# Selective scan's fourth silu of a block, from behind the gathered experts' gelu to in front of it in ScalarE's order

## What is computed

```python
# selective scan
xs, gate = jnp.split(h @ W_in, 2, axis=-1)
xs = silu(causal_conv(xs) + conv_b)                 # 512 channels, kernel 4
delta = mean(softplus(xs @ Wd + bd), axis=-1)
dA = exp(delta * A);  Bx = (xs @ B_mat.T) * delta
hs = scan(h = dA * h + Bx)
y = (hs @ C_mat.T + D_vec * xs) * silu(gate)
out_1 = x + y @ W_out
# experts: 8 heads, one of 4096 experts each
indices, scores = product_key_top1(x @ Wq.T, keys)
gate = relu(scores)
lin = (x . in_a[indices]) * gate
hidden = gelu(x @ W_in.T + sum_h lin * in_b[indices])
lout = (hidden . out_a[indices]) * gate
out_2 = hidden @ W_out.T + sum_h lout * out_b[indices]
```

## Time and profile before

| | |
|---|---|
| median of 3 runs | 4099.81 us (4099.64 to 4100.76) |
| the profiled execution's own time | 4113.66 us |
| its span, first to last instruction | 4111.9 us |
| TensorE busy, and its mean granted clock | 3689.5 us (90%), 0.943 of full speed |
| VectorE busy | 2578.5 us (63%) |
| ScalarE busy | 1742.1 us (42%) |
| GpSimd busy | 1087.5 us (26%) |
| the woven part of layer 1 in the span | about 1017 to 2110 us |

### The profile page before, as it was taken

The page is one execution under the profiler, slowest core; times in us unless marked ns, Lnnn a source line. Parts: engine busy times, 40 slices in busy tenths (PEclk is TensorE's granted clock), DMA queues, the critical chain, the costliest instruction groups (busy, mean ns, idle before and its releaser), DMA issues.

```text
span 4111.9 us, 47352 instructions
## 1 busy us (share of the span) xinstructions
PE 3689.5 (90%) x16820; PEld 2091.3 (51%) x16820; DVE 2578.5 (63%) x6523; ACT 1742.1 (42%) x3213; POOL 1087.5 (26%) x1140
## 2 busy tenths in 40 slices
PE   8899999787999898898859999999899999999997
PEld 7477777445544444454435555565543443444332
DVE  3534343646888977787754344442587888778881
ACT  2344333232343334333423333332226766666767
POOL 0611111602555545454512222222111010011001
PEclk7999999888999999899979999999899999999999
DMA  4356554204555646555510000000000000000000
GB/s 153 136 173 207 202 203 159 78 29 138 185 186 188 209 155 185 183 188 181 185 69 3 0 0 1 1 0 0 21 1 1 1 1 1 16 6 1 1 1 21
DMA packets 96157, 356.61 MB, mean 87 GB/s; under 512 B 15440, under 2 KB 42720, under 8 KB 85936
## 3 DMA queue, kind: packets, MB, share of 16 engines
q0 software_dynamic: 57328, 301.90, 22.6%
q1 hardware_dynamic: 37504, 49.58, 3.6%
q10 hardware_dynamic: 1088, 2.10, 0.1%
HBM read 322.32 MB, written 31.20 MB: 86 GB/s over the span
## 4 chain that ended last, share of the span: by engine, by line
PE 62%; DVE 24%; ACT 7%; issue 3%; POOL 3%; DMA 1%; POOLq 0%; SPq 0%; ACTq 0%; DVEq 0%
PE ps L171 48%; PE ps L2414 5%; DVE pm L2592 4%; PE ps L1947 2%; DVE gathB L1606 2%; PE ps L1429 2%; DVE hacc L1590 2%; ACT P L2743 2%; DVE mi L1548 2%; DVE ps L2595 1%; POOL xs_sorted L1147 1%; DVE tm L1506 1%; DVE fa L1856 1%; PE ps L2000 1%; DVE mx L1544 1%
## 5 line engine op out<-in xcount | busy, mean ns | idle before, releaser
L2743 ACT ACTIVATE P<-ps 128x512 f32<-128x512 f32 (+3 forms) x1280 | 589.2, 548 | 202.2 <-PE ps L171 199.5
L2592 DVE TENSOR_REDUCE pm<-ps 128x1 f32<-128x512 f32 x768 | 484.1, 685 | 82.1 <-PE ps L171 78.8
L1745 POOL DMA_INDIRECT gathB<-in_tab,idx x256 | 280.9, 1097 | 455.7 <-PE ps L1429 386.5
L2791 POOL TENSOR_SCALAR_AFFINE_SELECT P<-P 128x256 f32<-128x256 f32 x256 | 103.3, 407 | 911.0 <-ACT P L2743 907.1
L1745 POOL DMA_INDIRECT gathA<-in_tab,idx x256 | 272.8, 1066 | 226.9 <-DVE gte L1562 149.3
L171 PE MATMUL ps<-KS,QS 64*128 64x512 f32 (+3 forms) x1280 | 304.2, 424 | 21.4 <-DVE QS L2575 4.9
L2414 PE MATMUL ps<-P,Va 128*32 128x512 f32 (+3 forms) x2560 | 300.0, 541 | 11.3 <-POOL P L2791 6.3
L171 PE MATMUL ps<-QS,KS 64*128 64x512 f32 (+3 forms) x1280 | 283.4, 412 | 10.2 <-DVE xT L2543 4.6
L171 PEld LDWEIGHTS ps<-KS,QS 64*128 64x128 f32 x1280 | 139.7, 184 | 252.7 <-DVE pm L2592 69.5
L171 PE MATMUL ps<-f,K 128*128 128x512 f32 x1024 | 253.4, 399 | 13.9 <-POOL f L2205 11.3
L2595 DVE CUSTOM_DVE_ANT_0 ps<-ps,past 128x128 f32<-128x128 f32 (+3 forms) x512 | 240.7, 514 | 38.7 <-PE ps L171 37.6
(11 more groups left out here) (366 smaller groups left out, 7172.5 us busy)
## 6 DMA issues: line engine op xcount, KB each, us to landing
xs_sorted<-zero SPq DMA_DIRECT2D x1, 9088.0 KB, 33.0
xs<-xs_sorted SPq DMA_DIRECT2D x71, 128.0 KB, 2.2
ys_sorted<-ys SPq DMA_DIRECT2D x71, 128.0 KB, 1.7
gathA<-in_tab,idx POOLq DMA_INDIRECT x256, 5.5
gathB<-in_tab,idx POOLq DMA_INDIRECT x256, 5.1
out<-xT SPq DMA_DIRECT2D x8, 512.0 KB, 3.1
xT<-in_x SPq DMA_DIRECT2D x4, 512.0 KB, 9.6
xT<-in_x ACTq DMA_DIRECT2D x4, 512.0 KB, 8.6
```

The lines of the kernel that those rows point to most:

```text
L1745: pool.indirect_dma_start(out=(GA, GB)[half][:, h, :], out_offset=None, in_=d[f"tab{half}"], in_offset=bass.IndirectOffsetOnAxis(ap=idx[t ...
L2592: v = dve.tensor_reduce(m, p, AX.X, ALU.max)
L2743: act.activation(P_[:, hh, off:BW], psx.tile("s2", j, n, kt, pr, hh)[:, off:BW], ACT.Exp).then_inc(*psx.emptied(MN.act, "s2", j, n, kt, pr ...
L2791: pool.affine_select(out=P_, in_=P_, compare_op=ALU.is_ge, fill=0.0, base=0, pattern=[[0, 2], [1, 128]], channel_multiplier=-1).then_inc(* ...
```

## The change

In `act_mamba` the silu of round 6 (the fourth chunk) is emitted in slot 13, right behind the third chunk's, and no longer in slot 14. Slots 8 to 13 are as before, and so is the number of slots of a block. No instruction, wait or buffer is added or taken out in the program's text; table loads are placed by the compiler from the order.

```diff
@@ -1636,7 +1636,7 @@
                         yield from at.to((2, 3)[slot])
                     for i in range(7):
-                        yield from at.to(8 + i)
+                        yield from at.to(8 + min(i, 5))
                         if i < 4:
                             act.wait_ge(*MA.dve.has("halo", n))
                             act.wait_ge(*MA.pe.has("xs", n, i))
```

## The result

| | before | after |
|---|---|---|
| median of the runs that the prediction was set against | 4100.28 us (4099.64 to 4101.49, 4 runs) | 4072.39 us (4064.61 to 4075.00, 4 runs) |
| ratio, 95% interval | | 0.9928 [0.9911, 0.9946] |
| the profiled execution's own time, and its span | 4113.66, 4111.9 us | 4070.20, 4068.5 us |
| granted TensorE clock, mean | 0.943 | 0.949 |

The kernel is 27.9 us faster (22 to 36 by the interval); 33.9 us and 4065.9 us were forecast.

The account below looks back on a forecast made before the run. The fourth silu, queued behind the gelu's wait on ScalarE, was taken to stall TensorE, then VectorE. Gains of 9.7 + 9.4 + 8.4 + 6.4 = 33.9 us in blocks 3 to 6 gave 4065.9 us, range 4057 to 4075.

Parts of the forecast that it names:

- Where the order changes: Slot counts put the fourth silu ahead of the gelu in blocks 3 to 6 only; silu table loads 13 to 9.
- The silu's own cost: On ScalarE, cost 0, hidden in idle time; gelu not delayed, tightest in block 6 with 2.5 us to spare.
- Block 3, 9.7 us: TensorE's B starts 7.89 us earlier and, at full clock, takes 3.61 instead of 5.46, another 1.85 us.
- Block 4, 9.4 us: B follows routing groups 0 and 1, starting 7.45 us earlier, plus 1.99 us of clock.
- Block 5, 8.4 us: B starts at 1717.8 instead of 1724.17, 6.4 us earlier, plus 1.95 us of clock.
- Block 6, 6.4 us: B starts 6.4 us earlier; 4.4 us of idle time stay, and B is left at 4.91 us.
- What is late next: VectorE still waits about 1.2 us for block 3's group 2; transposes and gathers have slack, so the shift is kept.
- The check by the windows: Blocks 3 to 5 falling to block 2's length, plus block 6: 43.7 us, 4056.1, the gain's far end.
- Clock kept low: Rival: B stays slow after the shorter gaps, so 5.8 us of clock fall out: 4071.7 us; chance 0.08.
- Something else early: Rival: a gather or ScalarE's softplus is late next and takes a third: 22.6 us gained, 4077.2; chance 0.07.
- Loads only: Rival: only 5.1 us of table loads come off, 4094.7 us; chance 0.06 together with no order change.
- Slower: Rival: the silu's wait for the fourth convolution holds up the gelu, 31.6 us lost, 4131.4 us; chance 0.03.

Follow-up runs that it names:

- e3: Fourth silu moved in block 3 alone, blocks 4 to 7 as in the kernel before: 4102.30 us, ratio 0.9981 to the kernel before.
- e4: Fourth silu moved in block 6 alone, against the kernel before: 4104.37 us, ratio 0.9987.
- e5: Kernel before, old order, with a silu replacing the gelu of tiles 13, 17, 21 and 25, so without those table loads: ratio 0.9973 to the kernel before.
- e9: The changed kernel a third time, on another chip: 4147.07 us, ratio 0.9925 to the kernel before.
- e7: The changed kernel with block 7's third and fourth silu also in slot 12, in front of the gelu: ratio 0.9894 to the kernel before.
- e2: The kernel before, unchanged, run again against itself for a second trace: ratio 0.9997.
- e6: The changed kernel with another table loaded ahead of the fourth silu's wait in blocks 3 to 6: 4144.18 us, ratio 0.9901 to the kernel before.

## Why the prediction was right

**What bounds the kernel now: right.** The chain convolution, gelu's wait, silu, B, routing group 2 was the one that set the time. e3 and e4 show it block by block, e5 that it was the wait and not the loads.

**Where the order changes: right.** Blocks 3 to 6 and no other, 9 loads left, as the counts had it.

**The silu's own cost: right.** The gelu's load still starts 0.08 us after the last `hacc` ends (1420.06 + 4.68 = 1424.74, 1424.82). Block 6 was called the tightest, and there too the gelu was not held up: ScalarE still waits 2.44 us for its input after the silu.

**Block 3, 9.7 us: 9.8.** 7.89 us of start (16.77 ahead at B less 8.88 in block 2) and the slow B turned fast, 5.46 to 3.61.

**Block 4, 9.4 us: 12.0.** The term was too small, and its premise failed. B did not follow the routing groups without a wait (0.81 us idle), but TensorE reached them earlier: the products with `dg` before them had come after 2.75 us of idle time and run slowly, and now come after 1.25. Before, then after:

```profile
1563.33 1.63 PE L1429 MATMUL ps<-dg,gathB 128*128 128x128 f32 x8 [2.75 <-ACT dg L1708]
1564.76 1.92 PE L1429 MATMUL ps<-hg,gathB 128*128 128x128 f32 x8
```

```profile
1542.64 1.37 PE L1429 MATMUL ps<-dg,gathB 128*128 128x128 f32 x8 [1.25 <-ACT dg L1708]
1543.85 1.33 PE L1429 MATMUL ps<-hg,gathB 128*128 128x128 f32 x8
```

**Block 5, 8.4 us: 8.9.** The wait is 2.27 us where the prediction had 1.1, for the same reason (the products with `dg` ahead of it came after 2.82 us of idle time before, 1.25 now), and B is fast all the same.

**Block 6, 6.4 us: 5.1.** The start moved as said (4.29 us idle, 4.4 forecast), but B became slower than before, 6.35 against 4.91, with the clock at 0.50 in its first part; the prediction had left it as it was and named a slower B only as its worst case, at 0.69 us; it was 1.44. This term was too large.

```profile
1815.00:1820.00 5.00, 4.01 (x5) 0.73 (x6) 4.86 (x14) 2.24 (x3) 3.79 (x4) 0.50 0.85 275
```

**What is late next: right in its order.** The waits for group 2 are 1.20, 1.21 and 2.77 us in blocks 3 to 5, and 5.52 in block 6, where about 4 was said: the slower B is in it. TensorE's wait for `u` in the four blocks is 7.95 us, where "under 7" was said. The last gather of block 3 is issued at 1436.93, which is the trace's lead of 8.9 us and no more, and the `lin` products at 1445.21 start on ScalarE's `xt_`, as before; no gather became the bound.

**From the blocks to the median.** The sum for the four blocks, 33.9, stands against 35.7 in the first pair of traces and 33.2 between the mean woven parts (two traces of before, three of after 1086.5: 32.6). The three measured differences are 27.9, 36.3 and, for e9, 34.0 between medians. Why the first is smaller is not shown; its four runs span 10 us, and stages that the change doesn't touch vary by several us from run to run. The step that took the profile's sum over to the median one to one was right on average (the three have a mean of 32.7) and is good to about 6 us for one comparison. Part of the agreement is luck: blocks 4 and 6 missed in opposite directions, by 2.6 and 1.3 us in the first pair and by 1.3 and 2.1 in the second, so the sum is closer than its terms. The check by the windows, 43.7 us, was too large: block 5 kept a wait and B in block 6 became slower.

**The rivals.** Clock kept low: not in blocks 3 to 5; in block 6, where the sum had left B slow, it was slower still. Something else early: not seen. Loads only: refuted by e5. Slower: its condition never came near; in e7, where the fourth convolution of block 7 ends late, the gelu still waited 0.86 us for its own input.

## What to carry to other kernels

When two streams are woven into one in-order queue, look for a cheap instruction whose input is ready while the one ahead of it waits, and whose output an engine with more to do is idle for; its price is that engine's wait, not the instruction's or its table load's. Check a static weave over its whole length: two periods of 68 and 68.48 steps drift, so the same code is in one order in blocks 0 to 2 and in another in 3 to 6, and the blocks with the good order show what the others would take. After it, ask what is late next on that chain (here VectorE's convolution, worth about as much as one more block's stall).

## What the runs showed of the hardware that was not expected

A shorter gap doesn't mean a faster restart. B took 4.91 us after 10.76 us of idle time and 6.35 after 4.29, and in e2 4.93 after 6.03 and 6.43 after 8.61; the full speed is 3.61. Only after gaps of 2.43 us and less was B always at 3.61 (block 5 in six traces of the new order). Such a gap is no safe bound for other products: in block 2, after the same 2.47 us of idle time, the second group of products with the gathered rows took 1.86 us in the first trace of the kernel before (granted clock 0.57 from 1290.80 to 1294.00) and 1.33 us in e2 (1.00 from 1285.10 to 1288.00). The Trainium skill, page "TensorE: Matmul & The Clock Gate", section "HAM oscillation — how this bites in real kernels", has work after a long wait start at the low clock; the 0.50 after 4.29 us agrees, but how much of B falls into the slow stretch changes from one execution to the next (5.04 us in e9, after 5.05 us idle).

A table load can run ahead of the wait of the activation that needs it (e6, at 1500.78 for a wait that ended at 1505.00), while the gelu's load in the same trace ran behind its own wait (1509.65, after 4.01 us idle). What decides it is open.

Layer 0 takes 875 to 877 us on one chip and 945 to 951 on the other, for all kernels; the cause was not looked for.
